# Edge sums of a two-layer graph network: the routing matrices are made on ScalarE, four slots a relu, where VectorE made them with one compare-and-multiply each

## The reference, cut to what matters

```python
edge_index = jnp.stack([src, dst])
# first graph block                      # second graph block
gathered = A_values[:, None] * h[col]    msg = edge_val[:, None] * feat_in[edge_col]
agg = segment_sum(gathered, row, N)      aggr = segment_sum(msg, edge_row, N)
```

## Time and profile before

| | us |
|---|---|
| median of 3 runs (lowest, highest) | 3900.63 (3893.59, 3905.37) |
| span of the profiled execution | 3891.6 |
| first edge sum, first gather to last add | about 370 to 1552 |
| second edge sum, first gather to last add | about 1952 to 3147 |
| busy PE, DVE, ACT, POOL | 2650.3, 2586.9, 1024.1, 2179.1 |

### The profile page before, as it was taken

How to read it: one execution, slowest core, us unless ns; L and a number is a source line. 1 busy time by engine, 2 the same in 40 slices (tenths; PEclk the granted TensorE clock), 3 DMA queues, 4 the chain that set the end, 5 groups by cost and what they waited for, 6 DMA issues and landing times. The chain is left out here.

```text
span 3891.6 us, 55224 instructions
## 1 busy us (share of the span) xinstructions
PE 2650.3 (68%) x15016; PEld 2238.8 (58%) x15016; DVE 2586.9 (66%) x6599; ACT 1024.1 (26%) x2120; POOL 2179.1 (56%) x2145
## 2 busy tenths in 40 slices
PE   6886555444454545789946666666666657999998
PEld 4666343333343434689935444444444537999998
DVE  8997655444554555976746566666666677888886
ACT  0021000000000000567501111111111127888886
POOL 1434566666666664335456666666666603666665
PEclk8998777777777777899967777777887768999999
DMA  3011333333333332000133333333333334776775
GB/s 90 4 46 58 102 91 92 91 91 88 91 92 88 92 88 63 12 1 23 55 90 96 96 96 96 96 96 94 98 95 94 95 103 165 216 216 212 213 215 146
DMA packets 164219, 387.69 MB, mean 100 GB/s; under 512 B 46324, under 2 KB 95528, under 8 KB 150561
## 3 DMA queue, kind: packets, MB, share of 16 engines
q0 software_dynamic: 99072, 233.49, 22.0%
q1 hardware_dynamic: 64929, 151.65, 11.4%
HBM read 342.69 MB, written 42.97 MB: 99 GB/s over the span
## 5 line engine op out<-in xcount | busy, mean ns | idle before, releaser
L1089 POOL DMA_INDIRECT g_got<-table,e_source x1568 | 1493.5, 952 | 845.0 <-issue 440.0
L1115 DVE TENSOR_TENSOR A<-A,psum 128x256 f32 x1664 | 698.6, 420 | 876.3 <-remote 532.0
L1182 PE MATMUL psum<-g_got,g_route 128*128 x3328 | 1034.7, 473 | 141.0 <-DMA g_got<-table,e_source 74.2
L1182 PEld LDWEIGHTS psum<-g_got,g_route 128*128 128x128 f32 x3328 | 771.9, 241 | 329.0 <-issue 198.4
L786 PE MATMUL psum<-ident,g_rows 128*128 128x128 f32 x208 | 63.0, 401 | 663.3 <-ACT A L834 410.2
L1098 DVE TENSOR_SCALAR g_route<-columns,e_local,e_weight 128x128 f32<-128x128 f32 x1664 | 471.6, 362 | 17.4 <-issue 12.2
L786 PEld LDWEIGHTS psum<-ident,g_rows 128*128 128x128 f32 x208 | 29.7, 190 | 703.8 <-ACT A L834 505.7
L834 ACT COPY A<-psum 128x256 f32 x52 | 19.3, 372 | 999.4 <-issue 637.4
L369 POOL DMA_INDIRECT records<-rec,place x120 | 120.6, 1005 | 233.7 <-ACT rec L585 159.1
L140 PE MATMUL psum<-e_xt_hi,e_w_hi 128*128 128x256 f32 x832 | 238.2, 286 | 5.4 <-issue 5.2
L1612 POOL TENSOR_TENSOR f_ht_lo<-f_ht,f_ht_hi 128x512 fp32r<-128x512 f32 x100 | 134.2, 1347 | 181.1 <-ACT f_ht_hi L1551 174.6
(11 more groups left out here) (413 smaller groups left out, 5403.5 us busy)
## 6 DMA issues: line engine op xcount, KB each, us to landing
e_w<-in_m_w SPq DMA_DIRECT2D x104, 1024.0 KB, 5.1
g_got<-table,e_source POOLq DMA_INDIRECT x1568
expert_table<-g_normal SPq DMA_DIRECT2D x52, 128.0 KB
table<-xn SPq DMA_DIRECT2D x49, 128.0 KB
X<-in_x SPq DMA_DIRECT2D x1, 6144.0 KB
table<-f_ring SPq DMA_DIRECT2D x24, 256.0 KB, 2.1
out<-X SPq DMA_DIRECT2D x1, 6144.0 KB
f_w<-in_f_w SPq DMA_DIRECT2D x2, 1024.0 KB, 6.5
```

What stands on the lines that cost most here:

```text
L1089: pool.indirect_dma_start(got[:, c % RING, :], None, rows, bass.IndirectOffsetOnAxis(ap=source[:, c:c + 1].bitcast(U32), axis=0)).then_inc ...
L1115: dve.tensor_tensor(to, to, sums_of(c), ALU.add).then_inc(added, 1)
L1182: ins = pe.matmul(sums_of(c), route[:, c % (GB + GSEM), :], row(got, at[j % GSEM]), start=True, stop=True)
```

## The change

DVE makes no routes any more: its `make_routes` and the calls in `add_sums` and ahead of step 0 are gone. ACT makes them, in groups of four slots, in three stages in place: the square of (local target minus column number) for each slot, one relu of (1 minus square) over all four slots, which leaves 1 where the two are equal and 0 elsewhere, and a copy of each slot scaled by the edge's weight. Between the stages ACT waits on its own counter `hots_step`. Ahead of a group it waits until PE has used the group that stood five before in the ring. Seven groups are made ahead of the loop over the steps, and four in each pass of it, between the tile's work. In the first sum `keep_across` moves from the end of a pass to the place behind the next pass's `stage`. PE, POOL and SP keep their programs.

```diff
@@ aggregate, block.vector
-                    def make_routes(n, g):
-                        for j in range(g * GSEM, (g + 1) * GSEM):
-                            ins = dve.tensor_scalar(route[:, (n * GB + j) % (GB + GSEM), :], columns[:], local[:, n * GB + j:n * GB + j + 1],
-                                                    weight[:, n * GB + j:n * GB + j + 1], ALU.is_equal, ALU.mult)
-                        ins.then_inc(routed, 1)
...
-                        if n + 1 < STEPS:
-                            make_routes(n + 1, g)
...
-                    for g in range(GROUPS_OF):
-                        make_routes(0, g)
@@ aggregate, block.scalar
+                    def make_routes(group):
+                        if group >= STEPS * GROUPS_OF:
+                            return
+                        wait(act, pairs_summed, 2 * max(group - 4, 0))
+                        slots = range(group * GSEM, (group + 1) * GSEM)
+                        place = slots[0] % (GB + GSEM)
+                        of_group = route[:, place:place + GSEM, :].rearrange("p j n -> p (j n)")
+                        for c in slots:
+                            ins = act.activation(route[:, c % (GB + GSEM), :], columns[:], ACT.Square, bias=local[:, c:c + 1], scale=-1.0)
+                        ins.then_inc(hots_step, 1)
+                        before = 2 * (group + (STEPS * GROUPS_OF if through_mlp else 0))
+                        act.wait_ge(hots_step, before + 1)
+                        act.activation(of_group, of_group, ACT.Relu, bias=ones[:, 0:1], scale=-1.0).then_inc(hots_step, 1)
+                        act.wait_ge(hots_step, before + 2)
+                        for c in slots:
+                            to = route[:, c % (GB + GSEM), :]
+                            ins = act.activation(to, to, ACT.Copy, scale=weight[:, c:c + 1])
+                        ins.then_inc(routed, 1)
...
+                    else:
+                        act.wait_ge(edges.locals_made, 2)
+                        act.wait_ge(edges.weights_made, 2)
+                    for group in range(7):
+                        make_routes(group)
+                    before_tile = None
                     for n in range(1, STEPS):
+                        make_routes(4 * n + 3)
                         act.wait_ge(added, n * GB + 1)
                         t = tile_to_finish(n, mybir.EngineType.Activation)
                         tiles_of.tile.stage(act, n - 1, t)
                         if through_mlp:
+                            make_routes(4 * n + 4)
                             if n >= 2:
                                 tiles_of.keep_result(act, n - 2)
                             if n >= 4:
                                 tiles_of.keep_scores(act, n - 4, tile_to_finish(n - 3, mybir.EngineType.Activation))
                             if n >= 3:
                                 tiles_of.ln_root_of(act, n - 3)
+                            make_routes(4 * n + 5)
                             tiles_of.keep_turned(act, n - 1)
                             if n >= 2:
                                 tiles_of.root_of(act, n - 2)
+                            make_routes(4 * n + 6)
                             tiles_of.hide(act, n - 1)
                             if n >= 3:
                                 tiles_of.keep_normal_turned(act, n - 3)
                         else:
+                            if n >= 2:
+                                tiles_of.keep_across(act, n - 2, before_tile)
+                            before_tile = t
+                            make_routes(4 * n + 4)
+                            make_routes(4 * n + 5)
                             tiles_of.keep_turned(act, n - 1)
-                            tiles_of.keep_across(act, n - 1, t)
+                            make_routes(4 * n + 6)
+                    if not through_mlp:
+                        tiles_of.keep_across(act, FINISHES - 1, before_tile)
```

More of the change, by code:

```diff
@@ L1009, in build @@
         gathered = [sem(f"gathered{u}") for u in range(8)]
+        hots_step = sem("hots_step")
         def aggregate(rows, name, through_mlp, source, local, weight):
```

## The result

The changed kernel takes 3936.08 us (median of 4 runs, 3927.97 to 3946.98), the kernel before 3900.01 (4 runs): a ratio of 1.0095, 95% interval 1.0074 to 1.0116. It is 36 us slower. The profiled execution has a span of 3945.1 us, 53.5 above the one before. That is more than 36 because the profiled execution of the changed kernel is the slowest of its four (3946.98) and that of the kernel before the fastest of its own (3893.59); so the microseconds that are read from this pair of traces overstate the loss. I had forecast 3908.

A forecast was written before the change was run, and what follows sets the result against it. Gathers plus POOL's pause were taken to bound both sums, DVE's routes beside waits. Middles 0, first tail -1, second head +2, second tail +5: +6 to +7 on 3891.6, so 3898; runs' median 9.0 above the span, forecast 3908 us, range 3820 to 4000.

The forecast's parts named there:

- rival 1: Second sum slower because ACT's routes delay keep_result and keep_turned: 60 to 120 us more, 3960 to 4020 us; chance 0.27.
- The gathers and the pause set the period: Both sums: 16 gathers of 1.25 us plus 3.3 to 3.6 us of POOL waiting; DVE's routes are in neither.
- rival 3: Gathers were slowed by DVE's routes: at most 0.01 us each, 16 us in all, 3884 us; chance 0.02.
- A group of routes takes 3.44 us: On ACT: squares 1.26, scaled copies 1.26, relu 0.72, two own-counter waits of 0.1 us each; 13.8 us a step.
- First sum: 0 in the middle, -1 at head and tail: 7 us of cover hide a 5 us later turned-tile copy; head free, tail loses DVE's routes, -1 us.
- About 3 us of cover are left: Second sum: PE's turn matmuls end near +24 instead of +20.6; 49 periods cost 0, each further us beyond cover 49.
- the turned tile kept at +4.4 and `hide` at +8.7: Second sum: forecast times of ACT's tile steps, in us after the burst, with groups of routes between them.
- the burst: Both sums: PE's late completions reach the others together, some 2.8 us after the gather stream stops; cause unknown.
- Second sum's tail: +5: No gathers there: two steps took 32.5 us, 16.3 each; ACT needs 17.5 and some waits, 19: +5 us.
- Rival 2: Faster because PE's completions come sooner: pause wholly gone 323 us (3577), a fifth 65 us (3836); chance 0.21.
- My closing remark: Prediction's end: wrong above all if the burst's time depends on something other than the end of the gather stream.

The follow-up runs named there:

- e4: Changed kernel with ScalarE's tile work of a step put first in the second sum, one group of routes before hide, three behind; 3966.33 us, 1.0159 to the kernel before.
- e1: Kernel before with only the first sum's routes made by ScalarE as in the changed kernel; 3914.51 us, ratio 1.0028.
- e6: Kernel before plus the changed kernel's ScalarE order and groups, written to an unread tile, without waits on its own counter inside a group; 3936.74 us, ratio 1.0082.
- e2: Kernel before with only the second sum's routes made by ScalarE as in the changed kernel; 3924.52 us, ratio 1.0048.
- e3: Kernel before with VectorE making only the first five groups of routes of each sum, then only raising the counter (output wrong); 3923.88 us, ratio 1.0053.
- e5: Kernel before, VectorE making the real routes, plus the changed kernel's ScalarE order, groups and waits, written to an unread tile; 3947.39 us, ratio 1.0111.
- e8: Kernel before with a GpSimd memset of 1200 bytes a partition behind every two gathers; 4264.66 us, ratio 1.0927.
- e12: Kernel before plus the changed kernel's ScalarE order and pairs_summed waits, without the groups' work; 3505.52 us, ratio 0.9996, on a chip where the kernel before takes 3506 us.
- e9: Kernel before with a GpSimd memset of 400 bytes a partition behind every two gathers; 3864.81 us, ratio 0.9912.

## Why the prediction was right in its range and wrong in its size

The measured 3936 us lie within the stated range of 3820 to 4000, which was made wide for the rivals. They lie outside the forecast's own range (3885 to 3930) and below that of rival 1 (3960 to 4020): it falls between the two, where none of my sums had put it, and the range holds it by its width.

- *The gathers and the pause set the period, DVE's routes lie beside waits*: right. Without routes the sums are 6 us shorter and 3.5 longer; gathers take 947 ns on average after the change and 952 before. The 5 ns are 9 us of POOL's busy time in all, within the bound of rival 3, but no gain came of them: POOL's idle time grew by 62 us.
- *A group of routes takes 3.44 us, bounds 3.3 to 3.8*: right for the work, wrong for the waits. 4 x 390 less overlap, 722, and the copies make 3.27 us without a wait (in e4 three groups take the 9.81 us from 2648.42 to 2658.23). In the changed kernel a group takes 3.34 us in the median, but 4.84 on average in the first sum and 3.73 in the second, from the first square's start to the last copy's end. The sum had 0.1 us for each wait on the own counter; ahead of the relu it is 394.4 / 416 = 0.95 us on average and up to 8.8. The Trainium skill, "ScalarE: Activation LUTs", section "What ACT_TABLE_LOAD costs", would have one activation of 128 columns with its operand at 387 ns and the relu at 706; the trace agrees with 390 and 722. (A group comes to 3.24 us by its figures, not to the 3.25 that I had.) Its advice in "Rules for kernel authors" to keep such work on VectorE is borne out by the time of this kernel (1.0095), though not by the price of the operations.
- *First sum: 0 in the middle, -1 at head and tail*: the middle was right (548 gathers against 549), the head was not. I had written: "ACT has five groups in the ring before DVE is done clearing `A`, so no cost". It cost about 10 us there; e1 has 11 for the whole sum. e6 has the same head without the relu's wait and loses 3 gathers in the first 200 us where the change loses 7, so this wait is a part. The rest of it I did not separate. The tail took 30.1 us from the end of the last gather to the last add, before and after: 0, not -1.
- *Second sum: "About 3 us of cover are left. 49 periods: 0."* This is the step that failed: it put at 0 what came out as 41 us in the profiled execution and 19 us by e2's ratio. I reckoned with steps of ScalarE that shift by a few microseconds and stay covered, the turned tile kept at +4.4 and `hide` at +8.7. In the period shown they start at +10.6 and +22.1. A completion that falls into the last part of the stream is not late by what the step was late, but by what the hold adds (7.6 us there). `first_product` moved from just behind the burst to 13.5 us behind it (2411.98, against 2398.47), and its completion with it among the late ones. The price is below that of rival 1 (60 to 120 us), and its mechanism is in part the right one: between the adds of 2398.47 and the copy of the turned tile ScalarE makes three groups, two of them those that rival 1 named, ahead of `keep_result` and of `keep_turned`. But ACT kept idle time, of which rival 1 wanted hardly any (it is busy for 767.2 us of 1236). e4 shows that the order tried there is no cure.
- *Second sum's tail: +5*: the other way. From the end of the last gather to the last add it is 33.3 us where it was 36.3.
- *Rival 2, completions sooner*: POOL's pause did not go by this change. That it has to do with what DVE and ACT do in the first sum is not supported by e3 or e5 (549 and 548 gathers in the middle 800 us). It is gone when a gather comes every 1.74 us (e8), and on the chip of e12. By the earlier trace rows the burst comes 2.9 to 3.0 us after the last gather has ended, where I had read 2.8. My closing remark, that I would be wrong above all if the burst's time depended on something else than the end of the stream, points at the right place.

What stays open: whether the work in the groups or the waits for `pairs_summed` push `hide` back, why 13 waits at `hide` leave POOL's rhythm nearly whole in e3 and 20 to 24 do not, and what holds the completions at all. That the change would cost nothing where nothing is held is argued, not shown. The granted clock of the second sum (0.73 after, 0.77 in the earlier trace rows) is no explanation: e3 has 0.74.

## What to carry to other kernels

Before work is moved to an engine "with room", mark in the trace where in the period the completions are seen that its queue waits for: a step that slides from a prompt stretch into a held one can lose far more than it slid (here `hide` came 7.6 us behind its product instead of 1.9). Room in busy time says nothing on that. And where a stream of indirect DMAs is followed by a burst of late completions, a spaced stream is worth a trial: 0.46 us of idling behind every two gathers gained 0.9%, more than any moving of work here. Try it on more than one chip. On that of e12 POOL never stops, and there, by an estimate from e9's rows (two gathers in 2.80 us against 2.50), the same memsets would make each sum 392 x 0.30 = 118 us longer.

## What the hardware showed that I had not expected

- On the chips of the first eleven runs, completions of PE, and of ACT to itself, reach their waiters late while gathers follow one another every 1.25 us (7.6 us for one of `first_product`, 6.9 us for one of ACT's squares), and at once at 1.74 us. The gathers' data are not late: their last packets end 1.4 to 1.9 us after the gather in the 40 looked at.
- The same kernel takes 3900 us on the chips of the first eleven runs and 3506 us on that of the twelfth, with no held completion and a gather every 1.25 us throughout. The difference, some 394 us, is that of the two sums (192 and 199 us by the traces of the kernel before and of e12). What sets the chips apart no run shows.
